# Splitting the row maxima of two attentions into three bfloat16 parts on ScalarE and GpSimd instead of VectorE

## What is computed

```python
x = x + attn(layernorm(x))            # 16 heads of 16, 4 key/value heads, rotary positions, causal
x = x + xattn(layernorm(x), ctx)      # 16 heads of 16, keys and values from ctx, a mask on the keys
x = x + ffn(layernorm(x))             # 1024 hidden, relu, hidden and weights rounded to 4+3 bit floats
```

## Time and profile before

| | us |
|---|---|
| median of 3 runs | 1980.95 (1979.71 to 1982.15) |
| the profiled execution | 1985.14 |
| its span | 1983.5 |
| TensorE busy | 1792.5 (90%) |
| VectorE busy | 1391.6 (70%) |
| ScalarE busy | 865.7 (44%) |
| GpSimd busy | 643.4 (32%) |
| row maxima, VectorE L746, 448 | 538.8, 1222 ns each |
| the cut's four operations, VectorE L757 to L760, 64 each | 46.2, 24.8, 11.7 and 12.3 |

### The profile page before, as it was taken

How to read it: one execution, slowest core, us unless ns; L and a number is a source line. 1 busy time by engine, 2 the same in 40 slices (tenths; PEclk the granted TensorE clock), 3 DMA queues, 4 the chain that set the end, 5 groups by cost and what they waited for, 6 DMA issues and landing times.

```text
span 1983.5 us, 33931 instructions
## 1 busy us (share of the span) xinstructions
PE 1792.5 (90%) x12542; PEld 1036.3 (52%) x12542; DVE 1391.6 (70%) x2192; ACT 865.7 (44%) x1320; POOL 643.4 (32%) x698
## 2 busy tenths in 40 slices
PE   2879999999989999899999989999899999989897
PEld 1545555555545555555555545555555555545554
DVE  4668585785858768585885858768585786858662
ACT  3325344443444335344443544345344543544343
POOL 3241414324151251414324151252415324151300
PEclk9979999999999999999999999999999999999998
DMA  6370543725245270543725245270543725154230
GB/s 166 46 104 12 82 62 46 104 32 78 41 65 85 33 105 20 81 62 46 104 33 81 37 67 82 33 113 14 80 60 46 104 33 84 35 70 70 34 44 11
DMA packets 86606, 124.08 MB, mean 63 GB/s; under 512 B 10481, under 2 KB 53938, under 8 KB 86322
## 3 DMA queue, kind: packets, MB, share of 16 engines
q1 hardware_dynamic: 83650, 115.26, 41.5%
q0 software_dynamic: 2160, 7.87, 1.0%
q10 hardware_dynamic: 768, 0.57, 0.1%
HBM read 21.42 MB, written 8.39 MB: 15 GB/s over the span
## 4 chain that ended last, share of the span: by engine, by line
PE 56%; issue 19%; DVE 12%; POOL 6%; DMA 3%; ACT 2%; SPq 0%; POOLq 0%; ACTq 0%; DVEq 0%
PE small L1013 9%; PE o_ps L1174 7%; PE small L1237 6%; DVE negmax L746 5%; PE score L1139 5%; PE score L1096 5%; PE score L1101 4%; POOL P L469 3%; PE score L1066 3%; PE small L1268 3%; DVE xn L732 2%; DMA Q<-negT 2%; PE small L1284 2%; DVE negparts L757 2%; PE small L997 2%
## 5 line engine op out<-in xcount | busy, mean ns | idle before, releaser
L746 DVE TENSOR_REDUCE negmax<-score 128x4 f32<-128x1024 f32 (+1 forms) x448 | 538.8, 1222 | 124.9 <-PE score L1101 83.2
L570 ACT ACTIVATE P<-score 128x1024 f32<-128x1024 f32 x448 | 447.8, 1025 | 178.7 <-PE score L1116 105.1
L1174 PE MATMUL o_ps<-P,V 128*32 128x256 f32 (+1 forms) x4096 | 283.3, 363 | 25.1 <-POOL P L469 19.8
L781 DVE TENSOR_TENSOR P<-P,cross_bound 128x1024 f32<-128x1024 f32 x192 | 226.5, 1221 | 56.7 <-ACT P L570 50.8
L468 POOL TENSOR_TENSOR carrier<-minus_half 128x1 f32<-128x1 f32 x160 | 56.1, 351 | 644.4 <-ACT P L570 640.2
L1013 PE MATMUL small<-xnT,w 128*128 128x512 f32 x392 | 204.7, 665 | 5.2 <-ACT inT L527 2.7
L1096 PE MATMUL score<-K,Q 96*128 96x256 bf16 x1024 | 155.9, 274 | 56.3 <-issue 32.3
L1174 PEld LDWEIGHTS o_ps<-P,V 128*32 128x32 f32 x4096 | 86.4, 108 | 164.6 <-issue 72.8
L1139 PE MATMUL score<-Q,K 99*128 99x256 bf16 x1024 | 155.8, 275 | 7.5 <-DVE negmax L746 7.4
L408 POOL TENSOR_TENSOR rstd<-vareps,minus_half 128x4 f32<-128x4 f32 x48 | 55.0, 1146 | 307.3 <-DVE vareps L727 307.3
L1101 PE MATMUL score<-cross_q,identb 128*128 128x512 bf16 x512 | 154.2, 382 | 0.0
(11 more groups left out here) (141 smaller groups left out, 3034.4 us busy)
## 6 DMA issues: line engine op xcount, KB each, us to landing
Q<-q1p SPq DMA_DIRECT2D x96, 256.0 KB, 7.5
K<-k2p SPq DMA_DIRECT2D x96, 256.0 KB, 8.0
Q<-q2p SPq DMA_DIRECT2D x192, 128.0 KB, 5.0
x_in<-in_x SPq DMA_DIRECT2D x16, 512.0 KB, 7.8
ctxT<-in_ctx SPq DMA_DIRECT2D x16, 512.0 KB, 7.7
k2f<-q1f SPq DMA_DIRECT2D x32, 256.0 KB, 3.5
out_y<-x POOLq DMA_DIRECT2D x15, 512.0 KB, 4.8
K<-k1p SPq DMA_DIRECT2D x96, 64.0 KB, 7.3
```

What stands on the lines that cost most here:

```text
L570: A.activation(P[:, t % 4, :], score[b][:, :, :], ACT.Exp, scale=SCALE).then_inc(score_free[b], 1)
L746: V.tensor_reduce(negmax[:, k, h:h + 1024 // w], s.rearrange("p (h w) -> p h w", w=w), AX.X, ALU.max, negate=True).then_inc(score_free[b], 1)
L781: V.tensor_tensor(p, p, cross_bound[:, t % 2, :].unsqueeze(1).broadcast_to([128, 4, SEQ]), ALU.min).then_inc(probs_masked[1], 1)
L1174: last = T.matmul(o_ps[ob][32 * j:32 * j + 32, SEQ * gg + q0:SEQ * gg + SEQ], v, p, start=s == 0, stop=end, tile_position=(0, 32 * j), ski ...
```

## The change

`cut_max` is gone from VectorE. Its rounding steps are ScalarE's (`cut_first`, `cut_second`), its two differences GpSimd's (`cut_rest`, `cut_third`); part 1 is now rounded from the rest itself. The four steps count the same semaphore `neg_step` up by one each, so each waits for the one before on the other engine, and TensorE still waits for all four. `cut_first` also waits for the last two row maxima. The second half of a cut lies thus: in self attention, `cut_first` and `cut_rest` come before the exponentials and masks of E1, `cut_second` after the first exponential and `cut_third` after the first mask; in cross attention, `cut_first` is the first thing in the next body on ScalarE, `cut_second` stands behind the first exponential, and both differences are the first things in the next body on GpSimd. In its last lines a body on GpSimd now has the first half of the cross maxima between the differences and the third parts of q1 and k1.

```diff
--- before.py
+++ after.py
@@ -407,6 +407,19 @@
                 pool.wait_ge(ln_step[n], LN_STEPS * (g + 1))
                 G.tensor_tensor(rstd[:, :], vareps[:, :], minus_half[:, :], ALU.pow).then_inc(rstd_ready[n], 1)
 
+            def cut_rest(a, g, b):
+
+                blocks, at = slice(NBLK // GB * b, NBLK // GB * (b + 1)), NEG_STEPS * (GB * g + b)
+                pool.wait_ge(neg_step[a], at + 1)
+                G.tensor_tensor(negrest[:, blocks, :], negmax[:, blocks, :], negparts[a][:, blocks, 0:HEADS],
+                                ALU.subtract).then_inc(neg_step[a], 1)
+
+            def cut_third(a, g, b):
+
+                blocks, at = slice(NBLK // GB * b, NBLK // GB * (b + 1)), NEG_STEPS * (GB * g + b)
+                pool.wait_ge(neg_step[a], at + 3)
+                G.tensor_tensor(negparts[a][:, blocks, 2 * HEADS:3 * HEADS], negrest[:, blocks, :],
+                                negparts[a][:, blocks, HEADS:2 * HEADS], ALU.subtract).then_inc(neg_step[a], 1)
             def add_row(out, in_, row, ready):
                 for k in range(NBLK):
                     last = G.tensor_tensor(out[:, k, :], in_[:, k, :], row[:, :], ALU.add)
@@ -468,13 +481,6 @@
                 G.tensor_tensor(carrier[:, m:m + 1], minus_half[:, 0:1], minus_half[:, 0:1], ALU.add)
                 G.affine_select(out=p, in_=p, compare_op=ALU.is_ge, fill=0.0, base=0, pattern=[[0, heads], [1, 128]],
                                 channel_multiplier=-1).then_inc(probs_masked[0], 1)
-
-            def self_parts(g):
-
-                rest("q1", g)
-                rest("k1", g)
-                third("q1", g)
-                third("k1", g)
 
             pool.wait_ge(made, 13)
             inverse_root(0, 0)
@@ -488,9 +494,17 @@
 
             def body(i, prev, nxt):
                 st = BODY(i)
+                if prev:
+                    cut_rest(1, i - 1, 1)
+                    cut_third(1, i - 1, 1)
+                cut_rest(0, i, 0)
+                cut_third(0, i, 0)
+                cut_rest(0, i, 1)
                 for t in range(N1):
                     if bounded(0, t) is not None:
                         bound(i, t)
+                    if t == 0:
+                        cut_third(0, i, 1)
                     if prev and t == 1:
                         inverse_root(2, i - 1)
                     if nxt and t == 7:
@@ -504,7 +518,13 @@
                     rope_sum("q1", q1s, i + 1)
                     rope_products("k1", cosk, sink, k1s, i + 1)
                     rope_sum("k1", k1s, i + 1)
-                    self_parts(i + 1)
+                    rest("q1", i + 1)
+                    rest("k1", i + 1)
+                cut_rest(1, i, 0)
+                cut_third(1, i, 0)
+                if nxt:
+                    third("q1", i + 1)
+                    third("k1", i + 1)
                 if prev:
                     add_ffn(st, i - 1)
 
@@ -512,6 +532,8 @@
             with pool.Fori(1, NG - 1) as i:
                 body(i, True, True)
             body(NG - 1, True, False)
+            cut_rest(1, NG - 1, 1)
+            cut_third(1, NG - 1, 1)
             inverse_root(2, NG - 1)
 
 
@@ -550,6 +572,21 @@
                 t = full[name]
                 A.activation(parts[name][:, n], t[(slice(None),) * len(t.shape)], ACT.Copy).then_inc(done[name], 1)
 
+            def cut_first(a, g, b):
+
+                last = N1 // GB * (b + 1) - 1 if a == 0 else N2 // GB * (b + 1) - 1
+                for t in (last, last - 1):
+                    n, before = tile(("S1", "S2")[a], g, t)
+                    act.wait_ge(score_free[n], before + 1)
+                blocks = slice(NBLK // GB * b, NBLK // GB * (b + 1))
+                A.activation(negparts[a][:, blocks, 0:HEADS], negmax[:, blocks, :], ACT.Copy).then_inc(neg_step[a], 1)
+
+            def cut_second(a, g, b):
+
+                blocks, at = slice(NBLK // GB * b, NBLK // GB * (b + 1)), NEG_STEPS * (GB * g + b)
+                act.wait_ge(neg_step[a], at + 2)
+                A.activation(negparts[a][:, blocks, HEADS:2 * HEADS], negrest[:, blocks, :],
+                             ACT.Copy).then_inc(neg_step[a], 1)
             def exponentials(st, a, g, with_keys=False):
                 phase, n = ("E1", N1) if a == 0 else ("E2", N2)
                 done = 0
@@ -568,6 +605,8 @@
                     if positive(g * PVS + PV0[a] + t - 3):
                         act.wait_ge(pv_done, g * PVS + PV0[a] + t - 3)
                     A.activation(P[:, t % 4, :], score[b][:, :, :], ACT.Exp, scale=SCALE).then_inc(score_free[b], 1)
+                    if t == 0:
+                        cut_second(a, g, 1)
                     if t == 1 and with_keys:
                         keys(st, 0)
                     if t == 2:
@@ -645,13 +684,17 @@
             def body(i, prev, nxt):
                 st = BODY(i)
                 if prev:
+                    cut_first(1, i - 1, 1)
                     exponentials(st, 1, i - 1, with_keys=True)
                 else:
                     keys(st, 0)
+                cut_first(0, i, 0)
+                cut_second(0, i, 0)
                 keys(st, 1)
                 if prev:
                     turns(st, "oT2_", inT)
                 maxima(st, 0, 0)
+                cut_first(0, i, 1)
                 exponentials(st, 0, i)
                 if prev:
                     hidden(st, [0])
@@ -677,6 +720,8 @@
                 if nxt:
                     part("q1", 0, whole, part1, i + 1)
                     part("k1", 0, whole, part1, i + 1)
+                cut_first(1, i, 0)
+                cut_second(1, i, 0)
                 maxima(st, 1, 0)
                 if nxt:
                     part("q1", 1, rest1, part2, i + 1)
@@ -689,6 +734,7 @@
             with act.Fori(1, NG - 1) as i:
                 body(i, True, True)
             body(NG - 1, True, False)
+            cut_first(1, NG - 1, 1)
             exponentials(END, 1, NG - 1)
             for b in range(GB):
                 bk = END.bank(f"oT2_{b}")
@@ -745,19 +791,6 @@
                     k, h, w = t // 4, 4 * (t % 4), SEQ
                 V.tensor_reduce(negmax[:, k, h:h + 1024 // w], s.rearrange("p (h w) -> p h w", w=w), AX.X,
                                 ALU.max, negate=True).then_inc(score_free[b], 1)
-
-            def cut_max(a, g, t, b):
-
-                for last in (t, t - 1):
-                    n, before = tile(("S1", "S2")[a], g, last)
-                    dve.wait_ge(score_free[n], before + 1)
-                blocks, at = slice(NBLK // GB * b, NBLK // GB * (b + 1)), NEG_STEPS * (GB * g + b)
-                m, r = negmax[:, blocks, :], negrest[:, blocks, :]
-                p = [negparts[a][:, blocks, HEADS * k:HEADS * k + HEADS] for k in range(3)]
-                chain(V.tensor_copy(p[0], m), neg_step[a], at + 1)
-                V.tensor_tensor(r, m, p[0], ALU.subtract).then_inc(neg_step[a], 1)
-                chain(V.tensor_tensor(p[1], m, p[0], ALU.subtract), neg_step[a], at + 3)
-                V.tensor_tensor(p[2], r, p[1], ALU.subtract).then_inc(neg_step[a], 1)
 
             def normalise(st, a, u, g):
 
@@ -905,8 +938,6 @@
                         normalise(st, 1, 2 if t == 1 else 3, i - 1)
                     if t == 5:
                         values2(st, 0)
-                        cut_max(0, i, t, 0)
-                cut_max(0, i, N1 - 1, 1)
                 if prev:
                     if positive(16 * (i - 1)):
                         dve.wait_ge(y_stored, 16 * (i - 1))
@@ -953,9 +984,6 @@
 
                 for t in range(N2):
                     row_max(1, i, t)
-                    if t == N2 // 2 - 1:
-                        cut_max(1, i, t, 0)
-                cut_max(1, i, N2 - 1, 1)
 
             body(0, False, True)
             with dve.Fori(1, NG - 1) as i:
```

## The result

The changed kernel takes 1991.27 us (median of 5 runs, 1989.64 to 1992.33), the kernel before 1979.81 beside it. The ratio is 1.0056 with a 95% interval of 1.0041 to 1.0070, 11.5 us slower. I had forecast 22 us slower and a range from 1986 to 2019: the side and the place were right, the size twice too large. The profiled execution of the changed kernel took 1992.33 us with a span of 1990.3, against 1983.5 before, so its rows have 6.8 us to explain. That is less than the 11.5 of the medians: the profiled execution of the kernel before, 1985.14 us, is among the slowest of that kernel.

A forecast was written before the change was run, and what follows sets the result against it. TensorE, almost without gaps, was taken to set the pace. Stall less gain, 14 x (2.36 - 1.38), with small terms 13.6, clock at D +12, other clock -3: +22 us, 2003 us, range 1986 to 2019.

The forecast's parts named there:

- D: Last cut of the cross maxima, at the loop's end: TensorE stalls behind GpSimd's queue, 2.36 us lost an iteration.
- C: Cut in the middle of the cross maxima: TensorE's wait there goes, 1.38 us gained an iteration.
- A and B: The two cuts of the self maxima: the first gains 0.04 us an iteration, the second costs nothing.
- D and the clock: TensorE's gap at D lowers its clock in 9 of 14 iterations at 1.3 us: 12 us lost.
- The other clock drop: Clock drops in the stage before the cross scores: two fewer, 3 us gained.
- rival 1: Same stall at D, but the gap is too short for the clock to fall: about 1993 us; chance 0.24.
- Rival 2: At D, DMA issue and branch do not hold GpSimd, 1.17 us lost: 1978 to 1981 us; chance 0.07.
- Rival 3: D's stall spares the clock and the other stage keeps its clock in all 12 iterations: 1974.5 us; chance 0.06.
- Rival 4: More waits: covers at B or C fail, or VectorE's bound blocks GpSimd at D: 2020 us; chance 0.11.

The follow-up runs named there:

- d_before_add: The changed kernel with GpSimd's two differences of D at the end of the body, ahead of the ffn addition and its DMA: 1955.42 us.
- only_d: The kernel before with only cut D moved to ScalarE and GpSimd, the other cuts on VectorE: 2003.62 us.
- dma_late: The changed kernel with only the issue of GpSimd's DMA moved behind D's differences, the addition still ahead of them: 1974.90 us.
- abc: The changed kernel with cut D back on VectorE, the other three cuts moved: 1945.04 us.
- filled: The changed kernel with 7 extra products on TensorE ahead of its wait for D's parts: 1989.50 us.
- busier_before: The kernel before with 10 extra products on TensorE at the place of its wait for D's parts: 1994.41 us.
- only_c: The kernel before with only cut C moved to ScalarE and GpSimd, the other cuts on VectorE: 1951.79 us.
- abc_split: The changed kernel with D back on VectorE and GpSimd's ffn addition in four pieces of 128x256 instead of one: 1942.54 us.

## Why the prediction was right or wrong

The step that failed is the size of D's stall: the sum put 2.36 us an iteration on it, and the rows show 1.79. With 1.79 in its place the same sum gives 14 us, beside the 11.5 measured. The side, the place and the chain of waits were right.

**C**: forecast 1.38 us an iteration with 0.5 us of cover for the transposes, measured 1.40 with 0.7. Right.

**A and B**: forecast 0.04 and nothing, together 0.15. Right in kind. At B, GpSimd's last difference ended at 662.25, 0.65 us before TensorE's transposes at 662.90, where the sum had 0.5, and the exponentials were not late.

**D, the stall**: the mechanism was right and carried the sign; d_before_add shows it as directly as can be. Its size was wrong in two terms. The loop's branch on GpSimd was charged with 0.35 us, from VectorE's 0.31; L414 starts 0.03 us after the DMA's issue ends, so the branch adds nothing there. And ScalarE catches up faster than I had it: from L414 to the tile that now starts at 624.91 went 4.14 us, where my sum had 4.4. Together 0.57 us an iteration too much, 14 times 8 us, the largest miss of all terms. The lower bound of the branch, 0, was in the range of that term and would have given 17 us.

**D and the clock**: forecast 9 drops at 1.3 us in the loop, measured 7 at about 1.45 (119.25 against 117.8): 12 and 10 us. The 117.8 is worked out, since no iteration of the changed kernel is without a low clock; only_d has 1.5 to 1.7 directly. The gap was 1.62 + 0.30 us instead of 2.2 + 0.6, for the same reason. Over all traces the fall behind D in the loop came only with such a gap, but the same gap brought it in one iteration and not in another, for a cause that stays open; so that the count came out at 7, close to 9, is in part luck.

**The other clock drop**: forecast two fewer, 3 us; in the profiled execution 4 fewer, 6.7 us. The prediction called this luck, and it can be worth more than the change itself: from 12 drops of 1.67 us to 2 between kernels that differ by 1.45 us an iteration.

**The sum of the rows**: 14 x 0.3 for C, D, A and B is +4.2; 7 drops behind D +10.2; 4 fewer in the stage of xnT2 -6.7: +7.7 for the loop, and the 14 iterations of the two traces differ by 7.4 (1669.4 against 1662.0). After the loop the changed kernel takes 1.3 us more, with its second low stretch, and ahead of the cross scores of group 0 it took 1.9 less, which no term of mine explains: +6.8 between the two spans, +11.5 between the medians. The forecast had +13.6, +12 and -3.

**The range**: its upper end does not follow from what the prediction names for it. A clock falling in every iteration adds 6 us to 2003 and the dearer branch 5, which is 2014 and not 2019.

**The rivals**: rival 1 (the same stall without a clock loss, 1993) came nearest in time, but its reason is out: the clock fell, in half of the iterations. Rival 2 is out by the row of L414 and by dma_late. Rival 3's 9 spared drops did not occur here, only 4, though abc with its 10 shows that such a thing exists. Rival 4's lock is real (dma_late, d_before_add) and was absent at L414 in the changed kernel for the reason given. The Trainium skill's page "SBUF — State Buffer", section "SBUF: two separate sides", has the rule that such a mask and a GpSimd operation that reads SBUF block each other for a whole instruction; these rows agree: 1.23 us for L414 beside VectorE's mask, 0.26 without it.

## What to carry to other kernels

Work that is given to an idle engine should be looked at in that engine's queue, at the place where it will stand: at C, 0.5 us of work on GpSimd gained 1.4 us, at D the same work lost 1.8, for a 2.1 us addition and a DMA's issue that could as well have come after it, as d_before_add shows. A change that moves four pieces should be tried piece by piece, since here one piece hid another worth three times the sum. And where the clock of TensorE falls in some iterations, times of two kernels are compared only together with the count of these.

## What the runs showed of the hardware that I had not expected

The same matmuls in the stage of xnT2 at the low and at the full clock, in two iterations of the kernel before (TensorE's timeline):

```profile
580.53 3.57 PE L1013 MATMUL small<-xnT,w 128*128 128x512 f32 x4 [0.25 <-ACT inT L527]
```

```profile
818.96 1.98 PE L1013 MATMUL small<-xnT,w 128*128 128x512 f32 x4 [0.25 <-ACT inT L527]
```

What TensorE did before them, from 574.64 and from 813.06 on, is the same in both to 0.01 us, gaps included, and the clock fell in the one and not in the other. Whether it falls there goes by more than these last 6 us of TensorE's work. What was observed: in iterations of 119.2 to 119.5 us it tends to do in one what it did in the iteration before (12 of 14 low in the kernel before, 13 in filled, but 10 and 11 of 14 not low in busier_before and only_d, of the same length); at 116.0 us it mostly stayed high (2, 3 and 1 low of 14 in abc, only_c and abc_split); at 115.5 it was low in every second or third iteration. The lengths up to 119.5 include the drop where there was one. I tested no cause for this, and it stays open.

The branch at the end of the hardware loop cost GpSimd nothing visible here, behind the issue of a DMA: 0.03 us, against 0.31 on VectorE behind a short operation. Whether the engine or the issue makes the difference no run here shows.
